# A two-layer graph network on one Trainium2 core: where the nodes are finished, and which engine runs an unused branch's GELU

## The chip, the cores and the metric

The kernel runs on one core of one Trainium2 chip. The core's engines work side by side and meet only at semaphores: TensorE (PE in a profile: matmul, and its weight loads as PEld), VectorE (DVE), ScalarE (ACT), GpSimd (POOL) and SyncE (SP), which here only issues DMA transfers. The metric is the device time of one execution in microseconds (us). The kernel before has a median of 4388.27 us over three runs (4384.02 to 4390.1).

## The reference

There are 6250 nodes of 128 features and 206250 edges, sorted by destination (33 a node on average: 200000 drawn at random, and one self loop a node). Layer 0 is attention over edges and a feed-forward network, layer 1 a convolution over the same edges:

```python
# layer 0
m = leaky_relu(xl[src] + xr[dst] + edge_attr @ W_e, 0.2)
alpha = softmax of einsum(m, att) over the edges of each dst
h = layer_norm(x + segment_sum(xl[src] * alpha, dst) + b_att, g1, be1)
x = _layernorm(x + layer_norm(h + gelu(h @ W1 + b1) @ W2 + b2, g2, be2))
# layer 1, w00.. from a small network on edge_attr_8
n0, n1 = segment_sum(products of w, feat[src], edge_attr_4, dst)
y = cos * self(x) + sin * (n0, n1) @ W2
out = _layernorm(x + y)
```

All arithmetic that matters here is in float32.

## The kernel before, in words

Edges are taken in 403 groups of 512 (four tiles of 128). `program` calls stages one after the other, each a block in which every engine has its own instruction stream; a block ends when all of them have.

1. `set_up` makes the tables `xl` and `xr` and compares the destinations with fixed due groups. Its result `on_time` (with the test that no group spans too many nodes) goes into the flag `narrow`.
2. `attention` runs over the 403 groups. `by_width` branches on `narrow`: the narrow branch (`wins == 1`) has one window of nodes per group, the wide one (`wins > 1`) four. In the narrow branch the node updates of the first 14 x 384 nodes are done inside the loop as jobs (`job_on_pe`, `job_on_act`, `job_on_dve`): by then no later edge reaches those nodes. In the wide branch the jobs come after the loop. ScalarE's stream does not branch: its in-loop GELUs run in either case, and after its loop it runs `job_on_act(act, AFTER, ...)` for all 14 jobs with 4 GELUs each (L667). In the narrow branch TensorE opens these 56 with one `pe.sem_inc(hidden_ready, FC * JOBS)`, and what they write is not read.
3. `update_nodes` does the remaining nodes in two batches of 512.
4. `convolution` is the second loop. GpSimd gathers four tiles of rows per group by indirect DMA (L219) into a ring of eight groups; the gather of group k waits for `vals_ready` of group k-8. VectorE builds one-hot selectors (L1490) and the products (L1517 to L1528), ScalarE scales (L1465), TensorE makes the weights (L1441 to L1451) and sums by destination (L1434), and VectorE adds the sums to `acc` (L1503, L1505). A step of a stream works on several groups at once (TensorE on k to k-4, VectorE on k-3 and k-5).
5. `finish_nodes` comes after the whole loop, 13 batches of up to 512 nodes: TensorE turns `acc` (L1582) and multiplies (L1573, L1574), ScalarE copies the turned sums (L1595), VectorE adds, measures and normalises (L1614 to L1636), GpSimd takes the power -0.5 (L1604), SyncE stores.

The order in each engine's stream is that of the source: `steps` calls a body for every step, and nothing is reordered.

## Time and profile before

| | |
|---|---|
| median of three runs | 4388.27 us (4384.02 to 4390.1) |
| the profiled execution | 4350.94 us, of which the span from first to last instruction is 4348.8 us |
| busy in the span | PE 3377.7 us (78%), PEld 2309.2 (53%), DVE 3207.4 (74%), ACT 1823.7 (42%), POOL 3162.2 (73%) |
| instructions | PE 15016, DVE 10018, ACT 5130, POOL 3264 |
| mean granted TensorE clock | 0.947 of full |

Every time inside the kernel comes from the one profiled execution, which was 37.3 us (0.9%) shorter than the median of the timed runs. Busy shares are averages over stages with different limits; which engine is waited for must be read stage by stage. An engine's time may look idle in the page when it only issues a DMA, since issuing is not counted as busy for SP.

### The profile page before, as it was taken

The page shows a single profiled execution, that of the slowest core. Times are in us where ns is not written, and L with a number is a line of the kernel's source. Part 1 is how long each engine was busy: PE and PEld are TensorE (multiplying, and loading weights), DVE is VectorE, ACT ScalarE, POOL GpSimd, SP SyncE. Part 2 cuts the span into 40 slices and gives each one's busy share as a digit, 9 for nine tenths or more (in the row PEclk, how much of TensorE's full clock was granted, in tenths as well). Part 3 has the DMA queues.
Part 4 walks back from the last instruction along what each step waited for, and adds up shares of the span by engine and source line. Part 5 has one row for each costly group of instructions (what it writes and reads, how often), then busy time and mean ns, then how long its engine had stood idle before and what let it go on. Part 6 is the DMA issues. An engine that isn't in the chain of part 4 may idle for free. (4 is left out here: it accounts for less than half of the span.)

```text
span 4348.8 us, 64316 instructions
## 1 busy us (share of the span) xinstructions
PE 3377.7 (78%) x15016; PEld 2309.2 (53%) x15016; DVE 3207.4 (74%) x10018; ACT 1823.7 (42%) x5130; POOL 3162.2 (73%) x3264
## 2 busy tenths in 40 slices
PE   2878788877788878888567878777888877787776
PEld 2445455554455555554345556555555555555555
DVE  4557677777777767776567788788777787787877
ACT  1455565555555556555722222222222222222222
POOL 5677777777777777777267777777777777777773
PEclk7999999999998999999789999999999999999998
DMA  6655555555555555555112222222222222222221
GB/s 196 187 144 142 142 146 146 143 143 149 143 146 142 141 141 150 146 143 146 58 39 56 55 55 56 55 55 56 55 55 55 56 56 55 56 56 55 56 55 50
DMA packets 327847, 432.36 MB, mean 99 GB/s; under 512 B 132339, under 2 KB 217543, under 8 KB 327336
## 3 DMA queue, kind: packets, MB, share of 16 engines
q0 software_dynamic: 103168, 211.49, 18.6%
q1 hardware_dynamic: 224008, 216.62, 17.7%
q8 instruction: 131, 2.15, 0.2%
q14 instruction: 252, 2.06, 0.2%
q10 hardware_dynamic: 288, 0.04, 0.0%
HBM read 411.20 MB, written 16.65 MB: 98 GB/s over the span
## 5 line engine op out<-in xcount | busy, mean ns | idle before, releaser
L219 POOL DMA_INDIRECT ahead_rows<-feat,ahead_idx x1612 | 1580.8, 981 | 502.1 <-issue 490.7
L176 POOL DMA_INDIRECT ring_rows<-xl,ring_idx x1612 | 1542.6, 957 | 536.5 <-issue 514.8
L1434 PE MATMUL conv_sums_ps<-conv_vals,conv_onehot 128*128 128x256 f32 x3224 | 851.3, 409 | 415.0 <-DVE conv_vals L1528 414.9
L1465 ACT ACTIVATE conv_scaled<-conv_w_ps,c_xT 128x64 f32<-128x64 f32 x1612 | 374.9, 315 | 1451.5 <-PE conv_w_ps L1441 1451.5
L1434 PEld LDWEIGHTS conv_sums_ps<-conv_vals,conv_onehot 128*128 128x128 f32 x3224 | 604.4, 197 | 646.1 <-DVE conv_vals L1528 560.9
L1050 DVE SCALAR_TENSOR_TENSOR attn_leaky<-attn_pre_ps,c_b_r,attn_fifth 128x512 f32<-128x512 f32 x403 | 301.6, 748 | 431.8 <-ACT attn_fifth L930 424.7
L879 PE MATMUL attn_sums_ps<-attn_msg,attn_onehot 128*128 128x136 f32 x3224 | 478.4, 295 | 158.7 <-DVE c_acc_attn L985 155.3
L930 ACT ACTIVATE attn_fifth<-attn_pre_ps,c_b_r 128x512 f32<-128x512 f32 x403 | 276.2, 685 | 758.3 <-PE attn_pre_ps L870 748.1
L1517 DVE TENSOR_TENSOR c_W<-ahead_rows,c_xT 128x384 f32<-128x384 f32 x403 | 225.0, 558 | 407.8 <-DMA ahead_rows<-feat,ahead_idx 407.8
L879 PEld LDWEIGHTS attn_sums_ps<-attn_msg,attn_onehot 128*128 128x128 f32 x3224 | 427.0, 201 | 185.7 <-issue 177.9
L934 ACT ACTIVATE attn_far<-c_iota,c_dst_pos 128x128 f32<-128x128 f32 x1612 | 510.2, 390 | 0.6
L858 PE MATMUL attn_pre_ps<-c_xT,c_W_e 128*128 128x512 f32 x806 | 428.2, 613 | 51.8 <-DMA attn_xr_win<-xr_parts 51.8
L847 PE MATMUL attn_logit_ps<-attn_leaky,attn_att_pad 128*96 128x512 f32 (+2 forms) x806 | 439.2, 628 | 0.0
L1441 PE MATMUL conv_w_ps<-c_Wp,conv_hid 128*128 128x256 f32 x1612 | 436.3, 395 | 0.0
L870 PEld LDWEIGHTS attn_pre_ps<-c_ident,ring_rows 128*128 128x128 f32 x1612 | 191.8, 142 | 402.8 <-DMA ring_rows<-xl,ring_idx 302.9
L870 PE MATMUL attn_pre_ps<-c_ident,ring_rows 128*128 128x128 f32 x1612 | 253.9, 280 | 188.7 <-DMA ring_rows<-xl,ring_idx 188.4
L1490 DVE TENSOR_SCALAR conv_onehot<-c_iota,c_dst_pos 128x128 f32<-128x128 f32 x1612 | 363.6, 297 | 0.8 <-DVE c_acc_conv L1480 0.8
L1441 PEld LDWEIGHTS conv_w_ps<-c_Wp,conv_hid 128*128 128x128 f32 x1612 | 325.2, 202 | 51.5 <-ACT conv_hid L1471 1.0
L1451 PE MATMUL conv_hid_ps<-ahead_radial,c_mlp 16*128 16x256 f32 x806 | 280.7, 427 | 21.9 <-PEq L1063 21.9
L937 ACT ACTIVATE attn_onehot<-attn_far,c_one 128x512 f32<-128x512 f32 x403 | 290.9, 722 | 14.1 <-PE attn_sums_ps L879 1.0
L858 PEld LDWEIGHTS attn_pre_ps<-c_xT,c_W_e 128*128 128x128 f32 x806 | 154.4, 197 | 255.0 <-issue 200.1
L1044 DVE TENSOR_TENSOR attn_msg<-ring_rows,attn_turn_ps 128x512 f32<-128x512 f32 x403 | 271.9, 675 | 0.0
(214 smaller groups left out, 4505.9 us busy)
## 6 DMA issues: line engine op xcount, KB each, us to landing
c_xT<-in_attrT SPq DMA_DIRECT2D x403, 256.0 KB
attn_rel<-rel_group SPq DMA_DIRECT2D x403, 126.0 KB
ring_rows<-xl,ring_idx POOLq DMA_INDIRECT x1612
ahead_rows<-feat,ahead_idx POOLq DMA_INDIRECT x1612, 2.6
attn_xr_win<-xr_parts SPq DMA_DIRECT2D x403, 31.5 KB
ahead_radial<-in_radial_halves SPq DMA_DIRECT2D x101, 64.0 KB, 2.0
attn_limit<-limit SPq DMA_DIRECT2D x403, 16.0 KB
xr_parts<-set_parts SPq DMA_DIRECT2D x13, 384.0 KB, 3.4
```

What stands on the lines that cost most here:

```text
L176: pool.indirect_dma_start(self.rows[:, b, t, :], None, self.q["xl"][:, :], bass.IndirectOffsetOnAxis(ap=self.idx[:, s.slot(2), j * TG + t: ...
L219: pool.indirect_dma_start(self.rows[:, k.slot(U), t, :], None, self.q["feat"][:, :], bass.IndirectOffsetOnAxis(ap=self.idx[:, bass.ds(k.in ...
L847: nc.tensor.matmul(logit_ps[0:n * H, s.slot(2), :], att_pad[:, lo:lo + n * H], leaky[:, g.slot(2), :], start=j == 0, stop=j == n - 1).then ...
L858: nc.tensor.matmul(pre_ps[:, g.slot(2), :], sb["W_e"][:, :], attrT[:, b, :], start=True, stop=False)
L870: last = nc.tensor.matmul(pre_ps[:, g.slot(2), t * P:(t + 1) * P], xl_rows[:, g.slot(NX), t, :], ident[:, :], is_transpose=True, start=Fal ...
L879: last = nc.tensor.matmul(to, onehot[:, g.slot(2), t, :], msg[:, g.slot(2), t, :, :].rearrange("p h o -> p (h o)"), start=wins > 1 or t == ...
L934: nc.scalar.activation(far[:, t, :], sb["iota"][:, :], ACT.Abs, bias=sb["dst_pos"][:, bass.ds(g.index(TG, t), 1)], scale=-1.0).then_inc(fa ...
L1050: nc.vector.scalar_tensor_tensor(out=leaky[:, z.slot(2), :], in0=pre_ps[:, z.slot(2), :], scalar=sb["b_r"][:, 0:1], in1=fifth[:, z.slot(2) ...
L1434: last = nc.tensor.matmul(to, onehot[:, g.slot(2), t, :], vals[:, g.slot(2), t, :], start=wins > 1 or t == 0, stop=wins > 1 or t == TG - 1)
L1441: last = nc.tensor.matmul(w_ps[:, g.slot(2), c:TG:2, :], hid2[:, g.slot(2), c * P:(c + 1) * P], sb["Wp"][:, :, :], start=True, stop=True)
L1465: nc.scalar.activation(scaled[:, g.slot(2), t, :], w_ps[:, g.slot(2), t, 0:2 * MUL], ACT.Copy, scale=edge4[:, bass.ds(g.index(TG, t), 1), ...
L1490: last = nc.vector.tensor_scalar(onehot[:, g.slot(2), t, :], sb["iota"][:, :], sb["dst_pos"][:, bass.ds(g.index(TG, t), 1)], None, ALU.is_ ...
```

## The change

The ScalarE instructions after its attention loop are gone, with the `sem_inc` that opened them. In the wide branch the GELU of those jobs is now computed by VectorE with a rational approximation of erf (`gelu_on_dve`, 19 chained instructions and a last one for each chunk).

`finish_nodes` is gone. Its work is in `convolution`: for j = 0 to 10 in the narrow branch the pieces of batch j stand in the steps from 33 (j+1) + 8 on: TensorE's three (`fin_on_pe`: turn the first half, turn the second half, multiply) at offsets 0, 2 and 4, VectorE's four (`fin_on_dve`: two copies out of PSUM, add and measure, normalise) at offsets 1, 3, 5 and 6. Batch 11 stands in the last four steps and batch 12, of one tile, behind the loop. The reciprocal root is made on VectorE by three Newton steps (12 small chained instructions instead of GpSimd's one), the copies by VectorE instead of ScalarE. The result is normalised in place in `resid`, and SyncE stores all of it after its last radial load. `set_up` compares 12 further due groups and makes `narrow` false if one of them is late.

```diff
+FN = NB * P
+FIN_JOBS = -(-N // FN)
+FIN_EVERY = -(-E * FN // (N * GE))
+FIN_AFTER = 3
...
-                if done.at >= 1:
-                    act.wait_ge(gelu_ready, done.back(1).index(FC, c + 1))
...
-                    if wins == 1 and not k.turns and k.at == G + 3:
-                        pe.sem_inc(hidden_ready, FC * JOBS)
...
             steps(act, G, PEEL, U, TAIL, body, END, True)
-            for n in range(JOBS):
-                for u in range(U):
-                    job_on_act(act, AFTER, Step(JOBS + n), u)
...
                             job_on_dve(dve, AFTER, Step(0, i, 1, True), lambda: dve.wait_ge(acc_steps, 2 * wins * G), u)
+                            if U_HIDDEN <= u < U_HIDDEN + FC:
+                                gelu_on_dve(dve, AFTER, Step(JOBS, i, 1, True), u - U_HIDDEN, Step(0, i, 1, True))
...
+        def fin_settled(j):
+
+            return G if j == FIN_JOBS - 1 else (j + 1) * FIN_EVERY + FIN_AFTER
+
+        def fin_pieces(step):
+
+            found = []
+            for j in range(FIN_JOBS - 1):
+                u = step - fin_settled(j) - TAIL
+                if fin_settled(j) + TAIL + 7 <= G + TAIL:
+                    found += [(j, u // 2, None)] if u in (0, 2, 4) else []
+                    found += [(j, None, {1: 0, 3: 1, 5: 2, 6: 3}[u])] if u in (1, 3, 5, 6) else []
+                elif 0 <= u < 4:
+                    found.append((j, u if u < 3 else None, u))
+            return found
+
+        def fin_on_pe(pe, j, piece, settled):
+
+            if piece == 0:
+                pe.wait_ge(acc_steps, settled)
+            if piece < 2:
+                at_least(pe, fin_dve, j * FDS + FAT["turned0"] if piece else (j - 1) * FDS + FAT["turned1"])
+                for n, t in enumerate(fin_tiles(j)):
+                    last = nc.tensor.transpose(turn_ps[:, n, :], acc[:, t, piece * D:(piece + 1) * D], sb["ident"][:, :])
+            else:
+                pe.wait_ge(fin_dve, j * FDS + FAT["turned1"])
+                for n, t in enumerate(fin_tiles(j)):
+                    nc.tensor.matmul(out_ps[:, n, :], turned[0][:, n, :], sb["W_convA"][:, :], start=True, stop=False)
+                    last = nc.tensor.matmul(out_ps[:, n, :], turned[1][:, n, :], sb["W_convB"][:, :], start=False, stop=True)
+            last.then_inc(fin_pe, 1)
+
+        def fin_on_dve(dve, j, piece):
...
+            if piece < 2:
+                dve.wait_ge(fin_pe, j * FPS + (PE_TURN0, PE_TURN1)[piece])
+                at_least(dve, fin_pe, (j - 1) * FPS + PE_OUT)
+                nc.vector.tensor_copy(turned[piece][:, 0:n, :], turn_ps[:, 0:n, :]).then_inc(fin_dve, 1)
+            if piece == 2:
+                dve.wait_ge(fin_pe, j * FPS + PE_OUT)
+                nc.vector.tensor_tensor(v, out_ps[:, 0:n, :], v, ALU.add).then_inc(fin_dve, 1)
...
             steps(sp, G, PEEL, U, 0, body, written_out=True)
+            for j in range(FIN_JOBS):
+                sp.wait_ge(done_ready, j + 1)
+                if (j + 1) * FN <= N:
+                    sp.dma_start(out[j * FN:(j + 1) * FN, :].rearrange("(t p) f -> p t f", p=P), resid[:, j * NB:(j + 1) * NB, :]).then_inc(stored, 16)
...
-def finish_nodes(nc, sb, q, out, ahead):
...
-                finish_nodes(nc, sb, q, out, ahead)
```

ScalarE's stream between the attention loop and the second loop, before (each row is one or more instructions with their line; `attn_far` and `attn_onehot` are the loop's selectors, `upd_` tiles those of `update_nodes`):

```order
L934 ACTIVATE attn_far<-c_iota,c_dst_pos 128x128 x4
L937 ACTIVATE attn_onehot<-attn_far,c_one 128x512
L667 ACT_TABLE_LOAD
L667 ACTIVATE c_xT<-attn_pre_ps,c_b 128x384 x56
L502 UNCONDITIONAL_BRANCH
L1226 UNCONDITIONAL_BRANCH
L1243 ACTIVATE upd_hT<-upd_hT_ps,c_norm_columns 128x512
L1234 ACTIVATE c_acc_conv<-upd_hidden_ps,c_b 128x512 x4
```

The same place now, with the changed kernel's own line numbers (L994 was L934, L1293 was L1234):

```order
L994 ACTIVATE attn_far<-c_iota,c_dst_pos 128x128 x4
L997 ACTIVATE attn_onehot<-attn_far,c_one 128x512
L516 UNCONDITIONAL_BRANCH
L1285 UNCONDITIONAL_BRANCH
L1302 ACTIVATE upd_hT<-upd_hT_ps,c_norm_columns 128x512
L1293 ACT_TABLE_LOAD
L1293 ACTIVATE c_acc_conv<-upd_hidden_ps,c_b 128x512 x4
```

The 56 GELUs are gone, and the load of the GELU's table stands before the first GELU of `update_nodes`.

TensorE's stream at the end of the second loop's narrow branch, before (`conv_w_ps` and `conv_hid_ps` are the edge network, `conv_sums_ps` the sums of a group):

```order
L1434 MATMUL conv_sums_ps<-conv_vals,conv_onehot 128x256 x4
L1441 MATMUL conv_w_ps<-c_Wp,conv_hid 128x2x128 x2
L1447 MATMUL conv_hid_ps<-conv_hid,c_mlp 128x256
L1434 MATMUL conv_sums_ps<-conv_vals,conv_onehot 128x256 x4
L1441 MATMUL conv_w_ps<-c_Wp,conv_hid 128x2x128 x2
L1434 MATMUL conv_sums_ps<-conv_vals,conv_onehot 128x256 x8
```

The same place now (L1597 was L1434; `conv_turn_ps` holds turned sums, `conv_out_ps` the product for the output):

```order
L1597 MATMUL conv_sums_ps<-conv_vals,conv_onehot 128x256 x4
L1604 MATMUL conv_w_ps<-c_Wp,conv_hid 128x2x128 x2
L1501 MATMUL conv_turn_ps<-c_ident,c_acc_conv 128x128 x4
L1597 MATMUL conv_sums_ps<-conv_vals,conv_onehot 128x256 x4
L1501 MATMUL conv_turn_ps<-c_ident,c_acc_conv 128x128 x4
L1597 MATMUL conv_sums_ps<-conv_vals,conv_onehot 128x256 x4
L1505 MATMUL conv_out_ps<-c_W_convA,c_W 128x128
L1506 MATMUL conv_out_ps<-c_W_convB,c_node_rows 128x128
```

Batch 11's turns stand between the sums of the last groups; after the rows shown come its other three tiles and batch 12.

VectorE's stream at the same place now (L1673 and L1675 were L1503 and L1505; before, the two additions of each of the last groups followed one another with nothing between):

```order
L1698 TENSOR_TENSOR conv_vals<-conv_dot,conv_w_ps 128x4x32
L1521 COPY c_node_rows<-conv_turn_ps 128x512
L1666 TENSOR_LOAD c_tile_block
L1666 ISA x2
L1673 ISA
L1673 SCALAR_TENSOR_TENSOR c_acc_conv<-conv_sums_ps,c_keep,c_acc_conv 128x256
L1675 ISA
L1675 SCALAR_TENSOR_TENSOR c_acc_conv<-conv_sums_ps,c_pass_on,c_acc_conv 128x256
L1524 TENSOR_TENSOR c_acc_attn<-conv_out_ps,c_acc_attn 128x4x128
L1527 BN_STATS conv_stats<-c_acc_attn 128x6 x4
```

So VectorE adds batch 11's product before it adds the last group's sums.

## Rows read from the trace of the kernel before

**Rows 1.** The page; groups show count, busy us, mean ns, idle before and releaser.
```profile
span 4348.8 us, 64316 instructions
...
L219 POOL DMA_INDIRECT ahead_rows<-feat,ahead_idx x1612 | 1580.8, 981 | 502.1 <-issue 490.7
L176 POOL DMA_INDIRECT ring_rows<-xl,ring_idx x1612 | 1542.6, 957 | 536.5 <-issue 514.8
```

**Rows 2.** Waits in the second loop, 2230 to 4280 us: total us, times, longest.
```profile
POOL ahead_rows L219 <- issue: 485.8, 1594, 0.3
PE conv_sums_ps L1434 <- DVE conv_vals L1528: 413.1, 353, 2.9
DVE c_W L1517 <- DMA ahead_rows<-feat,ahead_idx: 406.6, 394, 1.8
```

**Rows 3.** Timeline of ACT at attention's end: start us, us, what.
```profile
2125.61 1.28 ACT L667 ACT_TABLE_LOAD   x1
2126.91 26.52 ACT L667 ACTIVATE c_xT<-attn_pre_ps,c_b 128x384 f32<-128x384 f32 x56
```

**Rows 4.** Timeline of DVE there; in brackets the idle time before.
```profile
2128.90 0.35 DVE L985 SCALAR_TENSOR_TENSOR c_acc_attn<-attn_sums_ps,c_pass_on,c_acc_attn 128x136 f32 x1
2153.74 0.52 DVE L1294 TENSOR_SCALAR c_W_convA<-c_W_convA 128x128 f32<-128x128 f32 x1 [24.49 <-PEq L502]
```

**Rows 5.** Timeline of ACT: first GELU of update_nodes, first table load of the loop.
```profile
2168.60 0.69 ACT L1234 ACTIVATE c_acc_conv<-upd_hidden_ps,c_b 128x512 f32<-128x512 f32 x1 [2.17 <-PE upd_hidden_ps L1198]
...
2224.16 1.28 ACT L1475 ACT_TABLE_LOAD   x1 [22.56 <-PE conv_hid_ps L1451]
```

**Rows 6.** Windows: length; PE, PEld, DVE, ACT, POOL busy; PEclk; DMA share; GB/s.
```profile
2153.70:2203.90 50.20, 26.11 (x112) 16.77 (x112) 29.42 (x95) 9.44 (x14) 24.25 (x16) 0.77 0.31 106
4287.10:4348.80 61.70, 38.94 (x312) 37.18 (x312) 40.58 (x182) 13.31 (x13) 13.14 (x13) 0.88 0.19 53
```

**Rows 7.** Groups by line from 4287 us on, columns as in rows 1.
```profile
L1573 PE MATMUL fin_conv_ps<-c_W_convA,fin_sumT 128*128 128x128 f32 x104 | 21.1, 285 | 5.8 <-DVE fin_v L1614 5.8
...
L1582 PE MATMUL fin_sumT_ps<-c_ident,c_acc_conv 128*128 128x128 f32 x104 | 15.3, 296 | 4.6 <-PEq L1367 3.5 <-ACT fin_sumT L1595 1.1
...
L1614 DVE TENSOR_TENSOR fin_v<-fin_conv_ps,c_acc_attn 128x512 f32<-128x512 f32 x13 | 9.0, 691 | 12.6 <-PE fin_conv_ps L1574 10.4 <-issue 1.7
```

**Rows 8.** Timeline of DVE and POOL in one attention job's normalising.
```profile
1966.82 0.17 DVE L686 TENSOR_SCALAR attn_spread<-attn_moments 128x3 f32<-128x3 f32 x1
...
1968.90 0.95 POOL L176 DMA_INDIRECT ring_rows<-xl,ring_idx  x1 [0.30 <-issue]
...
1969.14 0.16 DVE L698 SCALAR_TENSOR_TENSOR attn_rstd<-attn_error,attn_rstd 128x3 f32<-128x3 f32 x1
1969.33 0.88 DVE L704 TENSOR_SCALAR attn_v<-attn_v,attn_moments,attn_rstd 128x128 f32<-128x128 f32 x3
```

**Rows 9.** Timeline of all engines at the loop's end.
```profile
4278.03 1.29 POOL L219 DMA_INDIRECT ahead_rows<-feat,ahead_idx  x1 [0.30 <-issue]
...
4278.61 0.87 DVE L1490 TENSOR_SCALAR conv_onehot<-c_iota,c_dst_pos 128x128 f32<-128x128 f32 x4
...
4281.51 0.56 DVE L1517 TENSOR_TENSOR c_W<-ahead_rows,c_xT 128x384 f32<-128x384 f32 x1 [1.24 <-DMA ahead_rows<-feat,ahead_idx]
...
4283.72 0.28 DVE L1528 TENSOR_TENSOR conv_vals<-conv_dot,conv_w_ps 128x128 f32<-128x128 f32 x1
...
4284.06 1.99 PE L1434 MATMUL conv_sums_ps<-conv_vals,conv_onehot 128*128 128x256 f32 x8 [1.73 <-DVE conv_vals L1528]
...
4286.61 0.47 DVE L1505 SCALAR_TENSOR_TENSOR c_acc_conv<-conv_sums_ps,c_pass_on,c_acc_conv 128x256 f32 x1
```

**Rows 10.** Timeline of SP: the last radial loads, and the last store.
```profile
4170.12 61.57 SPq L213 DMA_DIRECT2D ahead_radial<-in_radial_halves  x4
...
4345.90 0.28 SPq L1654 DMA_DIRECT2D out<-fin_done  x1
```

**Rows 11.** The source line L219: landing of its transfers.
```profile
DMA to landing us min/median/max: 2.4/2.6/4.6
```

## What the change does to the time

> **What bounds the kernel now.** I read the page first. GpSimd's gathers are its two costliest groups: 1612 in each loop, with idle time that nothing but issuing fills [rows 1]. In the second loop the gathers take 981 ns and about 0.305 us of issue each (485.8 us in 1594 gaps), so a group of four costs 4 x 1.286 = 5.15 us, and 403 groups 2075 us. The waits of that loop say the same from the other side [rows 2]: GpSimd waits for no engine, while VectorE waits 406.6 us in 394 groups for gathered rows, 1.03 us each, and TensorE 413.1 us for VectorE's products. The reader is to see a loop in which GpSimd sets the pace and VectorE and TensorE each have about 1.03 us of room per group.
>
> Then I read the two places where no gather runs. At attention's end the timeline of ScalarE shows a table load and 56 GELUs from 2125.61 to 2153.43 us [rows 3]. VectorE finished its last addition at 2129.25 and began the next stage at 2153.74, after 24.49 us of idling [rows 4]. What ends last there is ScalarE, with work whose output nobody reads. After the second loop the last addition ends at 4286.61 + 0.47 = 4287.08 [rows 9], and the span ends at 4348.8: 61.7 us of `finish_nodes`, in which no engine is busy for more than 41 us and GpSimd for only 13 [rows 6].
>
> **The change part by part.**
>
> ScalarE's 56 GELUs. The next stage began 0.3 us after ScalarE's end (2153.43 to 2153.74). Without them the last to end is VectorE, at 2129.25, so the next stage begins at 2129.55: -24.2 us. The wide branch, with VectorE's GELU in it, is not executed, provided `narrow` holds (last rival). The table load goes with the 56 but comes back before the first GELU of `update_nodes`, as the order shows. There ScalarE waited 2.17 us for TensorE before that GELU, but a load that stands behind the wait is not hidden by it: at the second loop's start the load of 1.28 us begins after 22.56 us of waiting for a matmul, when that matmul is done [rows 5]. The whole stage waits for this GELU, so +1.3 us (bounds 0 and 1.3).
> The Trainium skill (ScalarE: Activation LUTs, What ACT_TABLE_LOAD costs) puts a change of tables at the load plus a drain of about 1.38 us, 2.66 us together, by which this term would be +2.7. The trace does not show the drain: the load takes 1.28 us and the next instruction starts 0.02 us behind it (2125.61 + 1.28 to 2126.91) [rows 3].
>
> `update_nodes` comes 24 us sooner after TensorE's idling. Its clock there was 0.77 of full, with 26.11 us of PE busy [rows 6]. TensorE now idles 24 us less before it, and at full clock 26.11 x 0.23 = 6 us could go. The order of events gives no reason why the granted clock must stay up, so I take 0, with bounds -6 and 0.
>
> `set_up` gets two small VectorE instructions. A small TENSOR_SCALAR takes 0.17 us [rows 8], so +0.3 us (bounds 0 and 0.3).
>
> Batches 0 to 10 in the loop. VectorE's cost for one: add, measure and normalise are the old stage's 40.58 us over 13 batches [rows 6], 3.1 us. The two copies out of PSUM are new to it; nearest is the addition of the same 128x512 from PSUM, 691 ns [rows 7]: 1.4 us. The root is a chain like the attention jobs' own: from 1966.82 to 1969.33, 2.5 us for 12 instructions, of which one is already counted [rows 8]: 2.3 us. Together 6.8 us a batch, in 33 groups that leave 33 x 1.03 = 34 us. TensorE's cost is 38.94 / 13 = 3.0 us, also against 34 us. So both fall behind for some seven groups and catch up long before the next batch. What decides is whether GpSimd notices. The gather of group k waits for the products of k-8. The last group's first gather began 3 x 1.25 before 4278.03, at 4274.3 [rows 9]. The products of group 394, which it had to wait for, were done eight groups before 4284.0, at 4242.8. There are 31 us of slack, and a delay of 6.8 us does not reach it. In these steps TensorE makes each piece while VectorE is a step behind, so the waits that are added find their work done or lose about a microsecond within the same lag. Behind the waiting VectorE instruction stand only the next group's one-hot and additions; what TensorE waits for there has the same slack. Cover: the gathers' 5.15 us a group. If it were gone, the 12 batches would cost 12 x 6.8 = 82 us.
>
> The gathers themselves. VectorE's work can lengthen them: the last gather, 1.29 us against a mean of 0.98, ran beside four one-hots [rows 9], and the mean of this loop, 981 ns, is 24 ns above that of the first, where one-hots are made elsewhere [rows 1]. Over a group that is 0.1 us for four one-hots. The normalising instruction is of the same kind, four to a batch, so 12 x 0.1 = 1.2 us; but beside a whole chain of an attention job a gather took 0.95 us [rows 8], which says 0. I take +1.0 (bounds 0 and 13; the upper one is 12 times the 1.1 us of one batch's four normalising instructions).
> The Trainium skill (SBUF — State Buffer, Who interferes with whom) speaks against this change: a VectorE `copy` or `tensor_scalar` in a two-port mode holds the port pair shared with GpSimd for the whole instruction, and descriptors of GpSimd's DMAs are not written meanwhile. By that rule every normalising instruction blocks, which is the second rival; by the rows it costs a tenth of that.
>
> The end of the loop. The products of the last group end at 4284.0. Before it VectorE has copied batch 11's first half in time for which it waited anyway (1.24 us idle before L1517 [rows 9]). Now: second copy 0.7 (4284.7); additions of group 401 0.9 (4285.6). TensorE finishes the last sums at 4286.05 and multiplies: 41.7 us over 13 batches (21.1 for L1573 and nearly as much for its partner), 3.2 us (4289.3). VectorE: add, measure and normalise 3.1, last additions 0.9, chain 2.3 (4295.6). Batch 12, one tile: two turns and copies, product, add and measure, then the chain of 2.5. I estimate 5.3 us from the chain plus eight short links of 0.3 to 0.4 (4300.9). The last store took 4348.8 - 4345.9 = 2.9 us [rows 10] (4303.8). So 4348.8 - 4303.8: -45.0 us (bounds -48, at TensorE's full clock throughout, and -41).
>
> The stores. SyncE issues eleven of them only after its last radial load, which lies at about 4231.7 [rows 10], 46 us before the last gather. They are 2.9 MB beside 55 GB/s of gathers. Landing takes 2.6 us and at most 4.6 [rows 11]; 2 us more for some groups is made up in the 1.03 us that each leaves. I take 0 (bounds 0 and 2). The last store waits for nothing but batch 12.
>
> Sum: -24.2 + 1.3 + 0.3 + 1.0 - 45.0 = -66.6 us. The span of 4348.8 becomes 4282.2 and the profiled execution of 4350.94 becomes 4284.3. The timed median stands 37.3 us above the profiled execution; since nothing in the profile says where these are, I carry them over unchanged: 4388.3 - 66.6 = 4321.7.
>
> **The rivals.**
>
> The boundary does not move. If something else ends attention, such as SyncE or a barrier that rows of instructions do not show, the 24.2 us stay and the table load doubles: 4388.3 - 66.6 + 24.2 = 4346. For it speaks only that SyncE's waits are not in a row; against it, that VectorE resumed 0.3 us after ScalarE. Chance 0.04.
>
> The gathers pay for each normalising instruction. 12 x 1.1 = 13 us instead of 1: 4334. For it the gather of 1.29 us, against it the gather beside the attention job. Chance 0.07.
>
> Slower than before: GpSimd is held for all of the VectorE time that is added. The place is the eleven batches in the loop and the twelfth in its last steps, the price 12 x 6.8 = 82 us in place of 1: 4388.3 - 66.6 + 81 = 4403. It decides from (66.6 + 1) / 12 = 5.6 us a batch. It needs either the ring's slack to be far below the 31 us that I read, or every kind of VectorE instruction to stop the gathers; [rows 2] and [rows 8] are against both. Chance 0.03.
>
> The change does not run as it says: one of the 12 new due groups is late, `narrow` is false, and the wide branches run. Each group then has six more additions of 0.47 us [rows 9], 2.8 us against 1.03 us of room, over 400 groups at least 700 us, so above 5000. From the reference's inputs I worked out the first destination of each due group: it lies 47 to 58 nodes past what is needed. Chance 0.01.
>
> **How the numbers follow.** The forecast, 4321.7, has 0.83. With the clock's 6 us and the spread of the timed runs (4 us) below it, and the costlier gathers, the slower landing and a longer end above it, its range is 4311 to 4340. That range holds the second rival too. The rest, 0.10, is the boundary (0.04), the two slow cases (0.04 together) and 0.02 for a gain that is lost in small pieces. A measurement of this kernel can tell about 0.2% (8.8 us) from no change. Faster takes the forecast and the first two rivals: 0.94; same 0.02; slower 0.04.
>
> **What would show it.** ScalarE without an activation between about 2125 and 2140, and VectorE resuming within 1 us of its last addition. The first GELU of the next stage behind a load of 1.28 us. In the second loop GpSimd still waiting for issue alone, mean gather 981 to 985 ns, and VectorE's wait for rows down by about 82 us, to some 325. From the last addition of group 402 to the end 12 to 13 us. The forecast is wrong if GpSimd waits for the products anywhere, if the mean gather rises above 990 ns (15 us in 1612), or if stores late in the loop push the last rows' landing back by more than 3 us.

## The result, and the profile after

The changed kernel takes 4324.22 us (median of 4 runs, 4321.41 to 4328.42) against 4386.15 us for the kernel before (4 runs, 4379.48 to 4390.1): -61.9 us, ratio 0.9875 with the interval 0.9848 to 0.9901. The forecast was 4321.7 us. The profiled execution took 4323.39 us with a span of 4321.6. Before's own profiled execution took 4350.94 us, so the two traces differ by only 27.2 us of span while the timed medians differ by 61.9; what lengthens the second loop in the one trace and not in the other is most of what follows.

The kernels below were timed in four further series; in three of them the mean granted clock of TensorE was 0.81 and the kernel before took 5628 to 5730 us (median), so each kernel is compared only with the runs of the kernel before in its own series.

The page's span and its two costliest groups, which answer to [rows 1]:

```profile
span 4321.6 us, 64148 instructions
...
L228 POOL DMA_INDIRECT ahead_rows<-feat,ahead_idx x1612 | 1617.5, 1003 | 504.6 <-issue 490.3
L185 POOL DMA_INDIRECT ring_rows<-xl,ring_idx x1612 | 1543.4, 957 | 535.6 <-issue 516.1
```

The first loop's gathers are as they were. Those of the second loop, 981 ns before, take 1003 now: 36.7 us more in 1612, and still nothing but issuing in GpSimd's idle time. The waits of the second loop, 2230 to 4280 us, answer to [rows 2]:

```profile
POOL ahead_rows L228 <- issue: 477.5, 1566, 0.3
PE conv_sums_ps L1597 <- DVE conv_vals L1698: 395.6, 310, 4.1
DVE c_W L1687 <- DMA ahead_rows<-feat,ahead_idx: 368.0, 343, 2.9
...
POOL ahead_rows L228 <- DVE conv_vals L1698: 0.6, 2, 0.3
```

GpSimd waited for the products 0.6 us in all: the slack of the ring held. VectorE's wait for rows fell by 39 us and not by 82, because the gathers themselves became longer. The boundary between the two loops answers to [rows 3] and [rows 4]: ScalarE's timeline, then VectorE's.

```profile
2124.20 0.72 ACT L997 ACTIVATE attn_onehot<-attn_far,c_one 128x512 f32<-128x512 f32 x1
2143.37 0.78 ACT L1302 ACTIVATE upd_hT<-upd_hT_ps,c_norm_columns 128x512 f32<-128x512 f32 x1 [18.44 <-PE upd_hT_ps L1275]
2144.16 1.28 ACT L1293 ACT_TABLE_LOAD   x1
2146.31 0.69 ACT L1293 ACTIVATE c_acc_conv<-upd_hidden_ps,c_b 128x512 f32<-128x512 f32 x1 [0.86 <-PE upd_hidden_ps L1257]
```

```profile
2128.30 0.35 DVE L1042 SCALAR_TENSOR_TENSOR c_acc_attn<-attn_sums_ps,c_pass_on,c_acc_attn 128x136 f32 x1
2131.38 0.52 DVE L1353 TENSOR_SCALAR c_W_convA<-c_W_convA 128x128 f32<-128x128 f32 x1 [2.73 <-PEq L516]
```

VectorE resumes 2.73 us after its last addition in place of 24.49. The table load stands ahead of the wait for `upd_hidden_ps`: after 1.28 us of loading ScalarE still waits 0.86 us for TensorE. The stage that follows, up to the first gather of the second loop, answers to the first of [rows 6], and the landing of the loop's transfers to [rows 11]:

```profile
2184.89 1.05 POOL L228 DMA_INDIRECT ahead_rows<-feat,ahead_idx  x1 [10.71 <-DMA feat<-c_acc_conv]
```

```profile
2131.38:2184.89 53.51, 28.65 (x112) 18.24 (x112) 29.22 (x95) 10.73 (x15) 24.28 (x16) 0.69 0.28 100
```

```profile
DMA to landing us min/median/max: 2.4/2.6/4.1
```

The stage is 2.4 us longer than the 51.14 us from VectorE's resuming to the first gather before. The end answers to [rows 9] and [rows 10]: the last gather (GpSimd's timeline), then VectorE's last addition for group 402, and SyncE's last store.

```profile
4295.37 0.95 POOL L228 DMA_INDIRECT ahead_rows<-feat,ahead_idx  x1 [0.30 <-issue]
...
4308.51 0.48 DVE L1675 SCALAR_TENSOR_TENSOR c_acc_conv<-conv_sums_ps,c_pass_on,c_acc_conv 128x256 f32 x1
...
4318.85 0.26 SPq L1572 DMA_DIRECT2D out<-c_acc_attn  x1
```

From the end of that addition to the end of the span are 12.7 us. The three stretches of the two traces, cut at the starts of the first and the last gather of the second loop (us):

| | before | after | difference | forecast |
|---|---|---|---|---|
| to the first gather | 2204.88 | 2184.9 | -20.0 | -22.6 |
| first to last gather | 2073.15 | 2110.5 | +37.3 | +1.0 |
| last gather to the end | 70.8 | 26.3 | -44.5 | -45.0 |

Two of the three are right within 3 us. The middle one is not, against this profile of before.

### The profile page after: what moved, and what is told of

Its sections match the earlier page's. It is cut to its first block and busy times, and to the rows that moved or that the text cites. A ratio compares the mean times of both kernels' runs of the same rounds, so it can differ in the third digit from the quotient of the medians.

```text
span 4321.6 us, 64148 instructions
## 1 busy us (share of the span) xinstructions
PE 3400.2 (79%) x14998; PEld 2321.5 (54%) x14998; DVE 3238.5 (75%) x10180; ACT 1785.1 (41%) x5061; POOL 3186.6 (74%) x3251
## 5 line engine op out<-in xcount | busy, mean ns | idle before, releaser
L228 POOL DMA_INDIRECT ahead_rows<-feat,ahead_idx x1612 | 1617.5, 1003 | 504.6 <-issue 490.3
L1597 PE MATMUL conv_sums_ps<-conv_vals,conv_onehot 128*128 128x256 f32 x3224 | 862.7, 414 | 402.9 <-DVE conv_vals L1698 402.1
L1597 PEld LDWEIGHTS conv_sums_ps<-conv_vals,conv_onehot 128*128 128x128 f32 x3224 | 613.4, 200 | 627.1 <-DVE conv_vals L1698 532.0
L994 ACT ACTIVATE attn_far<-c_iota,c_dst_pos 128x128 f32<-128x128 f32 x1612 | 510.8, 391 | 0.6
```

Source lines behind the costliest of these rows:

```text
L228: pool.indirect_dma_start(self.rows[:, k.slot(U), t, :], None, self.q["feat"][:, :], bass.IndirectOffsetOnAxis(ap=self.idx[:, bass.ds(k.in ...
L994: nc.scalar.activation(far[:, t, :], sb["iota"][:, :], ACT.Abs, bias=sb["dst_pos"][:, bass.ds(g.index(TG, t), 1)], scale=-1.0).then_inc(fa ...
L1597: last = nc.tensor.matmul(to, onehot[:, g.slot(2), t, :], vals[:, g.slot(2), t, :], start=wins > 1 or t == 0, stop=wins > 1 or t == TG - 1)
```

## Experiments

Three explanations of the longer gathers were tested. **Theory A**: a gather that starts beside VectorE's products is held until the group's one-hots are done whenever VectorE goes from one to the other with no idle time. The batches bring this about by making VectorE late; and before's own executions differ by how often it happens. **Rival B**: the added normalising and copying instructions themselves hold gathers. **Rival C**: the gap between before's profile and its timed runs has nothing to do with gathers. The first half of A, VectorE's lateness, is borne out below; the second, the one-hots, is not (see "Which instructions hold the gather").

### What the changed kernel's trace shows

VectorE and GpSimd around the normalising of batch 1 and two groups behind it (group 79 to 80):

```profile
2611.36 1.23 DVE L1552 TENSOR_SCALAR c_acc_attn<-c_acc_attn,conv_moments,conv_rstd 128x128 f32<-128x128 f32 x4
2611.59 0.94 POOL L228 DMA_INDIRECT ahead_rows<-feat,ahead_idx  x1 [0.30 <-issue]
2612.38 0.88 DVE L1660 TENSOR_SCALAR conv_onehot<-c_iota,c_dst_pos 128x128 f32<-128x128 f32 x4
2612.84 1.04 POOL L228 DMA_INDIRECT ahead_rows<-feat,ahead_idx  x1 [0.30 <-issue]
...
2617.93 0.56 DVE L1687 TENSOR_TENSOR c_W<-ahead_rows,c_xT 128x384 f32<-128x384 f32 x1
2618.39 0.29 DVE L1689 TENSOR_TENSOR conv_scal<-conv_w_ps,ahead_rows 128x128 f32<-128x128 f32 x1
2618.59 0.29 DVE L1691 TENSOR_TENSOR conv_dot<-c_W 128x128 f32<-128x128 f32 x1
2618.63 2.42 POOL L228 DMA_INDIRECT ahead_rows<-feat,ahead_idx  x1 [0.30 <-issue]
...
2620.13 0.29 DVE L1698 TENSOR_TENSOR conv_vals<-conv_dot,conv_w_ps 128x128 f32<-128x128 f32 x1
2620.33 0.88 DVE L1660 TENSOR_SCALAR conv_onehot<-c_iota,c_dst_pos 128x128 f32<-128x128 f32 x4
```

Beside the four normalising instructions, of 1.23 us together, the gather takes 0.94 us, and in the whole trace the 20 gathers that overlap such an instruction take at most 0.95: they cost nothing, against rival B. The long gather comes in group 80 (2618.63 us; it ends at 2621.05, just before the one-hots' end at 2621.21 and 0.6 us behind that of the last product at 2620.42), when VectorE has been late for two groups and starts its products with no idle time (no bracket behind the row at 2617.93). A gather of 2.4 us stands in the same place behind each of the eleven batches (groups 47, 80, 113, ... 377). The gathers of these eleven groups are 1.9 us longer each than the same ones in the trace of before, 21 of the 36.7 us; the other 16 are spread over the loop.

### The kernel before, profiled again

> The kernel before, unchanged, profiled once more. Its first profile has gathers of 981 ns in the second loop and an execution of 4350.9 us, 37 us under its own timed median; the changed kernel's has 1003 ns and no such gap. Theory A (the length of the gathers is unsteady in both kernels, and the first profile of before caught a short case): a second profile can come out at up to 4388 us, and then with gathers of up to 981 + 37000/1612 = 1004 ns. Theory C (the gap has nothing to do with the gathers): a longer execution with gathers still at 981 ns, the time elsewhere. Theory B (the change alone lengthens the gathers): 981 ns whatever the execution's time.

Measured: 5725.6 us against 5713.0 in the same series (ratio 1.0006, 0.9976 to 1.0035). None of the forecasts' times applies, but the run shows the hold plainly. The window 3500 to 3530 us, then a piece of VectorE's and GpSimd's timeline in it:

```profile
3500.00:3530.00 30.00, 29.50 (x121) 21.37 (x120) 30.00 (x108) 11.79 (x48) 25.73 (x15) 1.00 0.14 39
```

```profile
3503.71 2.42 POOL L219 DMA_INDIRECT ahead_rows<-feat,ahead_idx  x1 [0.30 <-issue]
...
3505.24 0.92 DVE L1490 TENSOR_SCALAR conv_onehot<-c_iota,c_dst_pos 128x128 f32<-128x128 f32 x4
3506.03 0.50 DVE L1503 SCALAR_TENSOR_TENSOR c_acc_conv<-conv_sums_ps,c_keep,c_acc_conv 128x256 f32 x1
...
3506.44 0.94 POOL L219 DMA_INDIRECT ahead_rows<-feat,ahead_idx  x1 [0.30 <-issue]
...
3507.69 2.42 POOL L219 DMA_INDIRECT ahead_rows<-feat,ahead_idx  x1 [0.31 <-issue]
```

VectorE is busy for all 30.00 us, catching up after it had stood still, and gathers of 2.42 and 0.94 us alternate. The long one starts at 3503.71 beside the products and ends at 3506.13, within 0.1 us of the end of the one-hots (3505.24 + 0.92). That the two ends coincide here does not yet make the one-hots the cause. There is no batch in this kernel's loop, so the hold occurs in the kernel before as well. Mean gather of this run: 1141 ns.

> The kernel before, unchanged, profiled a third time. In its second profile (5727 us) ScalarE and VectorE stood still for up to 31 us at a time with nothing that the trace names, and gathers took 2.42 us each wherever VectorE caught up without a gap. If that belongs to the hour and not to the kernel, this run is back near 4386 us. Theory A (the gathers' length is unsteady): an execution between 4350 and 4390 us whose mean gather in the second loop lies between 981 and 1004 ns in proportion. Theory C: near 4388 us with gathers of 981 ns. Theory B: 981 ns, and an execution near 4351 us.

Measured: 5644.7 us against 5628.4 (1.0024, 0.9995 to 1.0053), mean gather 1156 ns: the same picture, and no answer between A and C.

> The kernel before, profiled once more beside its own runs, which lay between 4346 and 4367 us in the hour of the finer-cut version and between 4379 and 4390 us beside the first result, while its first profile took 4350.9 us. Theory A (its gathers are held in some executions and not in others): an execution above 4360 us has a mean gather above 987 ns in the second loop, about 0.62 ns for each us above 4351, with gathers of 2.0 to 2.6 us later than the loop's start; one near 4351 us has 981 ns and none. Theory C: the mean gather stays at 981 ns whatever the time.

Measured: 5718.7 us against 5729.7 (0.9989, 0.9965 to 1.0013), mean gather 1092 ns. So no profile of before at 4360 us or more exists, and what makes its executions lie at 4346 to 4367 us in one series and 4379 to 4390 in another is not settled.

### One part alone

```diff
-                    if wins == 1 and not k.turns and k.at == G + 3:
-                        pe.sem_inc(hidden_ready, FC * JOBS)
...
-            for n in range(JOBS):
-                for u in range(U):
-                    job_on_act(act, AFTER, Step(JOBS + n), u)
```

> The first part of the change alone: the kernel before without the 56 GELUs on ScalarE and the semaphore increment behind them. By the prediction's step: -24.2 + 1.3 = -22.9 us against before. By the changed kernel's trace the table load is hidden before the wait: about -24 us. If what is saved at the boundary comes back in the loop (TensorE's clock, gathers in another phase): -10 to 0 us. The gathers' length in the second loop should be that of the kernel before by each theory.

Measured: 5685.6 against 5713.0 us (0.9955, 0.9935 to 0.9974): -27 us, interval -37 to -15. What VectorE waited for at the boundary (total us, times, longest), in this kernel and in the second profile of before:

```profile
DVE c_W_convA L1289 <- PEq L502: 2.7, 1, 2.7
```

```profile
DVE c_W_convA L1294 <- PEq L502: 22.6, 1, 22.6
```

> The first part alone once more (the kernel before without the 56 GELUs on ScalarE), since before took 5713 us in the hour of its first run. By the changed kernel's trace the next stage begins 22.4 us sooner (GpSimd's first instruction there 2131.36 in place of 2153.73 us) and the second loop's first gather 20.0 us sooner (2184.89 in place of 2204.88): -20 to -24 us against before, plus or minus what the gathers' length does in either, up to 37 us by the two profiles of before and of the changed kernel. By the prediction's step: -22.9.

Measured: 5701.7 against 5729.7 us (0.9960, 0.9938 to 0.9983): -28 us, interval -36 to -10. Both intervals hold the forecast's -22.9, and the wait of 2.7 us comes back. The gathers' lengths in these runs (1160 and 1154 ns) are those of the catching-up and say nothing about this part.

The other part alone is the changed kernel with these lines put back:

```diff
+                if done.at >= 1:
+                    act.wait_ge(gelu_ready, done.back(1).index(FC, c + 1))
...
+                    if wins == 1 and not k.turns and k.at == G + 3:
+                        pe.sem_inc(hidden_ready, FC * JOBS)
...
+            for n in range(JOBS):
+                for u in range(U):
+                    job_on_act(act, AFTER, Step(JOBS + n), u)
```

> The second part alone: the changed kernel with the 56 GELUs on ScalarE put back. By the prediction's steps: +1.0 + 0.3 - 45.0 = -43.7 us against before. If the batches in the loop lengthen gathers as the changed kernel's profile has it against the first of before (+36 us) and before's own timed runs do not have this: about -10 us. Theory A (before's timed runs have long gathers too): -38 to -44 us. In its profile the long gathers stand at the same place of each period of 33 groups as in the changed kernel, if the batches make them.

Measured: 5661.6 against 5713.0 us (0.9903, 0.9877 to 0.9929): -55 us by the ratio, interval -70 to -41. The forecast of -43.7 is inside, the "-10" of a kernel that pays all 36 us is outside. From the end of the last addition to the end of the span this kernel takes 12.8 us, where the three further profiles of before take 61.6 to 61.9: that is the gain at the loop's end. Its long gathers do not stand at one place of each 33 groups, as the changed kernel's do, but where VectorE catches up. In this kernel's loop TensorE, ScalarE and VectorE stand still for up to 34, 31 and 22 us at a time, under which some of GpSimd's extra time may be free, so the run bounds the cost of longer gathers only here.

### All batches behind the loop

```diff
-                    if wins == 1:
-                        for j, _, piece in fin_pieces(k.index()):
-                            if piece is not None:
-                                fin_on_dve(dve, j, piece)
...
-                for j in range(FIN_JOBS - 1 if wins == 1 else 0, FIN_JOBS):
+                for j in range(FIN_JOBS):
```

(and the same for TensorE)

> The changed kernel with all 13 batches made behind the loop, one after the other, none in it. What the loop hides comes due: 12 batches of 6.8 us of VectorE alone, 10 with the hops between engines, so 82 to 120 us more than the changed kernel, less what the gathers get back. Theory A: the long gathers at one place of each 33 groups are gone, mean gather 3 to 20 ns under the changed kernel's 1003. Theory B (each normalising or copying instruction of VectorE holds a gather): the same place is clean, mean gather 981, 36 us given back, so 46 to 84 us more than the changed kernel. Theory C: 1003 ns stays.

Measured: 5793.5 against 5713.0 us (1.0131, 1.0097 to 1.0164), so +75 us against before, and 132 us more than the kernel above, which has the batches in the loop and 24 us of GELUs besides. From the end of the last addition of the loop to the end of the span, with the 13 batches one after another:

```profile
5658.74:5812.10 153.36, 67.46 (x294) 57.84 (x294) 79.45 (x342) 0.00 (x0) 0.00 (x0) 0.62 0.07 22
```

11.8 us a batch: more than the 6.8 to 10 of the expectation. VectorE is busy for 6.1 us of them and TensorE, at 0.62 of its clock, for 5.2 in place of the 3.0 of the prediction, and here the two mostly take turns. The cover that the loop gives the batches is real. Its mean gather, 1131 ns, lies among those of its series (1108 to 1160), so it does not tell A from B.

### The changed kernel again, and the batches in finer pieces

> The changed kernel, unchanged, beside the kernel before of the same hour, for the whole change against the two parts measured in the first call (-26 and -55 us). If the parts add up: -75 to -85 us. By the changed kernel's own timing: -62 us (ratio 0.9875). If the parts share a gain: under -62 us.

Measured: 4316.0 against 4364.4 us (0.9902, 0.9871 to 0.9932): -48 us, less than in the first pair, and not the sum of the parts of another series (-27 and -55 us of 5713). Before's seven runs in this series lie at 4346 to 4367 us, the changed kernel's four at 4315 to 4319. The changed kernel is steadier between the two series (medians 4324 and 4316) than before (4386 and 4364). In before's two shortest runs (4346 and 4349 us) the mean granted clock was 0.949, in its five others 0.935 to 0.943. No trace of these five exists, so whether the clock, the gathers or both make them longer is open.

The finer pieces (`scale` is two of the four normalising instructions; the main lines of the edit):

```diff
...
-                    found += [(j, None, {1: 0, 3: 1, 5: 2, 6: 3}[u])] if u in (1, 3, 5, 6) else []
+                    fine = {1: [0], 3: [1], 5: ["v"], 6: ["stats"], 7: ["moments"], 8: [("root", 0)], 9: [("root", 1)], 10: [("root", 2)], 11: [("scale", 0)], 12: [("scale", 1)]}
+                    found += [(j, None, fine[u])] if u in fine else []
...
```

> The changed kernel with the pieces of a batch on VectorE cut finer and laid over steps 1, 3 and 5 to 12, so that none adds more than 0.9 us to a group that has 1.03 us to spare. Theory A: VectorE never has to catch up, so the gathers of 2.42 us at one place of each 33 groups are gone, 10 x 2 to 3 = 20 to 30 us less than the changed kernel (less where TensorE itself makes VectorE catch up). Rival B (each of the added instructions holds a gather for its own length): no difference, within 5 us. Rival C (nothing to do with gathers): no difference.

Measured: 4298.9 us (4293.1 to 4302.3) in the same series: 0.9859 of before (0.9828 to 0.9890), and 17 us less than the changed kernel, whose four runs lie above all four of this one. The loop's gathers, of the changed kernel in this series and of the finer pieces:

```profile
L228 POOL DMA_INDIRECT ahead_rows<-feat,ahead_idx x1612 | 1612.6, 1000 | 503.0 <-issue 490.6
```

```profile
L228 POOL DMA_INDIRECT ahead_rows<-feat,ahead_idx x1612 | 1597.0, 991 | 504.2 <-issue 489.9
```

15.6 of the 17 us are the gathers: the eleven groups behind the batches take 17.4 us less, all others together 1.8 us more. Gathers above 1.9 us are 22 where they were 30; behind the batches, four of the eleven places still have one, of 1.97 to 2.19 us, and five batches have one of 2.03 to 2.41 us one to three groups earlier. The same instructions are issued, only no more than about 1 us of them in a group: what costs is that VectorE becomes late, as theory A has it, and not the instructions. The forecast of 20 to 30 us was somewhat too high. This version beats both kernels.

### Which instructions hold the gather

One comparison of two tensors in place of the four one-hots:

```diff
-                        for t in range(TG):
-                            last = nc.vector.tensor_scalar(onehot[:, g.slot(2), t, :], sb["iota"][:, :], sb["dst_pos"][:, bass.ds(g.index(TG, t), 1)], None, ALU.is_equal)
-                        last.then_inc(onehot_ready, 1)
+                        nc.vector.tensor_tensor(onehot[:, g.slot(2), :, :], bc(sb["iota"][:, :], 1, TG), bc(sb["dst_pos"][:, bass.ds(g.index(TG), TG)], 2, P), ALU.is_equal).then_inc(onehot_ready, 1)
```

> The changed kernel with the four one-hots of a group as one VectorE instruction that compares two tensors (TENSOR_TENSOR with broadcast operands, 512 columns) instead of four TENSOR_SCALARs. Theory A with TENSOR_SCALAR as the one that holds: no gathers of 2.42 us, as in the version with ScalarE. If any VectorE work without a gap holds gathers: they stay at 2.42 us. The instruction itself may take 0.6 to 1.1 us against 0.87 for the four.

Measured: 4412.3 us in the same series as the last two (1.0129 of before, 1.0096 to 1.0162), 96 us more than the changed kernel. GpSimd and VectorE behind a batch:

```profile
2793.96 2.44 POOL L228 DMA_INDIRECT ahead_rows<-feat,ahead_idx  x1 [0.30 <-issue]
...
2795.50 0.28 DVE L1696 TENSOR_TENSOR conv_vals<-conv_dot,conv_w_ps 128x128 f32<-128x128 f32 x1
2795.70 0.68 DVE L1659 TENSOR_TENSOR conv_onehot<-c_iota,c_dst_pos 128x512 f32<-128x512 f32 x1
...
2796.30 0.47 DVE L1671 SCALAR_TENSOR_TENSOR c_acc_conv<-conv_sums_ps,c_keep,c_acc_conv 128x256 f32 x1
```

The comparison is shorter (0.68 us against 0.88), and the holds of 2.4 us are as long and as many: 29 gathers above 1.9 us against 30 in the changed kernel of this series. So the hold does not hang on TENSOR_SCALAR. It ends at 2796.40, with the comparison (2796.38), but also 0.62 us behind the last product (2795.78). What is new are gathers of about 1.43 us: 258 are above 1.3 us against 49, and 224 end 0.82 us behind the end of the comparison. The mean rises to 1054 ns, 87 of the 96 us: a comparison of two tensors lengthens gathers that the four one-hots leave alone. By the Trainium skill (SBUF — State Buffer, Who interferes with whom) a TENSOR_SCALAR in a two-port mode can keep descriptors from being written; a tensor_tensor with both inputs in SBUF contends with GpSimd's reads but, as the skill infers, not with the writing of descriptors. The rows show gathers of 0.94 us beside the normalising TENSOR_SCALARs and the longer ones beside tensor_tensors, so the first rule does not explain them; which of GpSimd's accesses is in the way no run here shows.

The one-hots on ScalarE, behind its GELUs, and taken out of VectorE's stream:

```diff
...
+                    for t in range(TG):
+                        nc.scalar.activation(onehot[:, g.slot(2), t, :], sb["iota"][:, :], ACT.Abs, bias=sb["dst_pos"][:, bass.ds(g.index(TG, t), 1)], scale=-1.0).then_inc(far_ready, 1)
+                    act.wait_ge(far_ready, g.uses(1, TG))
+                    nc.scalar.activation(onehot[:, g.slot(2), :, :], onehot[:, g.slot(2), :, :], ACT.Relu, bias=sb["one"][:, :], scale=-1.0).then_inc(onehot_ready, 1)
...
```

> The changed kernel with the four one-hots of a group made on ScalarE (4 of 0.39 and 1 of 0.72 us, as in the first loop) instead of on VectorE. Theory A, as it stands after the second profile of before (a gather that falls among VectorE's products is held until the group's one-hots, 2.42 us, when VectorE works without a gap, and the one-hots take part in it): no gather over 2 us, mean near 945 ns, 30 to 90 us less than the changed kernel where TensorE is not in the way. Rival B (the products hold the gather whatever comes behind them, or the normalising instructions do): gathers of about 2.4 us stay where VectorE catches up, the mean stays within 15 ns of the changed kernel's. If the products alone hold: the gathers get shorter by the 0.9 us of the one-hots, about 1.5 us instead of 2.42.

Measured: 5480.9 us (1.2556 of before, 1.2498 to 1.2614; three runs of 5462 to 5486 us, and a fourth of 18336 us that is left out and has no trace). The one-hots stand behind the GELUs in ScalarE's stream, so TensorE's sums wait for them, and the group takes 8.0 us. But the source line of its gathers (durations in ns; minimum, median, maximum) reads:

```profile
L228 POOL DMA_INDIRECT ahead_rows<-feat,ahead_idx x1612: 938/944/1320, 2183.2 to 5392.1; - x180
its engine sat idle before it (us, times) until:
  DVE conv_vals L1700: 1279.0, 386
```

1600 of 1612 gathers take 960 ns or less, with all the batches' copies, roots and normalising instructions still on VectorE (22 gathers overlap a normalising one, of 0.95 us at most): rival B is refuted. VectorE idles over half of this loop, so this run does not single out the one-hots. The same instructions ahead of `conv_scaled` in ScalarE's order:

> The changed kernel with the one-hots on ScalarE again, now ahead of conv_scaled in ScalarE's order instead of behind the GELUs, so that TensorE's sums need not wait for them. ScalarE's work for a group becomes 3.8 us, under the 5.0 us of four gathers. Theory A (only gathers beside VectorE's one-hots are held): every gather near 945 ns, with VectorE busy most of the time now, so 4 x (0.945 + 0.305) = 5.0 us a group and 85 to 90 us less than the changed kernel. If the gathers of 945 ns in the first version came from VectorE's idling (it was busy a good third of the loop): means of 970 to 1000 ns again, and 0 to 50 us less. If ScalarE's new work delays TensorE: slower than the changed kernel, with GpSimd waiting for conv_vals.

Measured: 5649.6 against 5729.7 us (0.9880, 0.9840 to 0.9919; a sixth run, of 11966 us and without a trace, is left out), -69 us by the ratio. The changed kernel is not in this series, so what the version would gain over it is open. VectorE's and GpSimd's timeline where VectorE catches up (from 3549.99 to 3554.7 it has less than 0.05 us of idle time at a stretch):

```profile
3549.99 0.48 DVE L1675 SCALAR_TENSOR_TENSOR c_acc_conv<-conv_sums_ps,c_keep,c_acc_conv 128x256 f32 x1 [0.54 <-PE conv_sums_ps L1598]
...
3551.50 0.94 POOL L228 DMA_INDIRECT ahead_rows<-feat,ahead_idx  x1 [0.31 <-issue]
...
3552.74 1.24 POOL L228 DMA_INDIRECT ahead_rows<-feat,ahead_idx  x1 [0.30 <-issue]
...
3554.29 1.27 POOL L228 DMA_INDIRECT ahead_rows<-feat,ahead_idx  x1 [0.30 <-issue]
```

Here gathers beside the products take 0.94 to 1.27 us. Elsewhere in the same loop, with no one-hots on VectorE, one takes 2.23:

```profile
3465.16 2.23 POOL L228 DMA_INDIRECT ahead_rows<-feat,ahead_idx  x1 [0.30 <-issue]
...
3466.50 0.28 DVE L1700 TENSOR_TENSOR conv_vals<-conv_dot,conv_w_ps 128x128 f32<-128x128 f32 x1
...
3467.66 0.48 DVE L1675 SCALAR_TENSOR_TENSOR c_acc_conv<-conv_sums_ps,c_keep,c_acc_conv 128x256 f32 x1 [0.89 <-remote]
```

It ends at 3467.39, 0.61 us behind the last product, while VectorE idles. Six of 1612 are like this one, of 2.23 to 2.36 us, where before's three profiles of such series have 124 to 203 above 1.9 us. So one-hots on VectorE are not needed for the hold, and the second half of theory A falls.

What the long gathers have in common can be counted over all 14 traces, which have 1343 above 1.9 us. Products here are a group's TENSOR_TENSORs from `c_W` to the `conv_vals` that reads `conv_w_ps` (rows 2617.93 to 2620.13 above), about 2.5 us. Every one started 0.66 to 1.14 us behind the start of a group's products, and ended 0.61 to 0.92 us behind the end of the last product. In the two versions without the four one-hots it is 0.61 to 0.63 throughout, in the others about 0.62, 0.79 or 0.91, so the four one-hots add 0.3 us at most. And of the gathers that started 0.65 to 1.05 us behind the products' start, none of 447 was held where VectorE idled for more than 0.05 us just before the products or among them, and 1314 of 1440 where it did not. That is VectorE's lateness in numbers: a late VectorE finds its rows landed and starts its products without a pause. Products also lengthen gathers that are not held: in the changed kernel's trace the 452 gathers that overlap no product take 949 ns on the mean and the other 1160 take 1025, in the second profile of before 945 and 1299.

In this version 79 of 95 such gathers met idling VectorE, which waited for ScalarE's part (236 waits before `conv_scal`), and 6 of the other 16 were held. That is the main reason why it has so few. Whether the one-hots raise the share of held ones (6 of 16 here, 182 of 193 in the second profile of before) is open.

The mean is 1003 ns against 1092 to 1156. The 945 that A named did not come: besides the six, 243 of 1612 gathers take 1.1 to 1.5 us.

## Why the prediction was right, and where it was not

The time came out within 2.5 us of the forecast, but one term of the sum was wrong by more than ten times its size in the traces, and a base that nobody had explained made up for it. The mechanism at the boundary and at the loop's end was right; that the time fits so closely is luck as far as the runs show.

- **The boundary, -24.2**: measured -22.4 (GpSimd and VectorE begin the next stage at 2131.4 in place of 2153.7). The mechanism is shown by the part alone (-27 and -28 us, and the wait down from 22.6 to 2.7). The size missed 1.8 us: between VectorE's last addition and its resuming lie 2.73 us, which before were hidden under ScalarE's work, and I had taken the 0.3 us that followed ScalarE's end; the last addition itself came 0.6 us sooner.
- **The table load, +1.3**: measured 0. From VectorE's resuming to the first GELU are 14.9 us in both traces. The step that said "a load that stands behind the wait" read the wrong order out of [rows 5]: here the load runs ahead of the wait and is hidden by it. The lower bound was right.
- **TensorE's clock in `update_nodes`, 0 (-6 to 0)**: outside the bounds. The granted clock of the stage is 0.69 where it was 0.77, TensorE is busy 28.65 us where it was 26.11, and the stage is 2.4 us longer. The difference lies near the stage's end: from 2173.4 to 2180.4 us the clock is 0.50, its lower level, and at the same place of before (2195.7 to 2202.7) it was 0.92. Less idling before a stage gave no faster clock in it.
- **Batches in the loop, 0**: right. GpSimd waited 0.6 us for products.
- **The gathers, +1.0 (0 to 13)**: this is the term that was mis-sized. Against the profile of before it is +36.7 us. Against before's timed runs it follows from the medians and the other two stretches: -61.9 + 20.0 + 44.5 = +2.6 us in the first pair, and -48.5 + 20.5 + 46.2 = +18 in the second (4314.2 - 4289.6 = 24.6 us from last gather to end there). I priced the instructions that could hold a gather and left out the lateness they cause, which carries gathers into the stretch of the products where they are held; the sentence "both fall behind for some seven groups and catch up long before the next batch" named the cause and gave it no price. The stated sign of failure, a mean gather above 990 ns, did appear. The rival of the normalising instructions named 13 us for the wrong reason: gathers beside them take 0.95 us at most, and the finer pieces keep all of them and lose 15.6 us.
- **The end of the loop, -45.0**: measured -44.5, with 12.7 us from the last addition where 12 to 13 were named. The part alone has 12.8 in place of 61.6 to 61.9.
- **The stores, 0**: landing took at most 4.1 us, as before (4.6).
- **The time**: 4324.2 against 4321.7; for the profiled execution the same sum gave 4284.3, and it took 4323.4. The base of 37.3 us between before's profile and its timed median was carried over as unexplained and fixed. It was not fixed: the changed kernel's profile and timed median agree within 1 us. That its gathers are 36.7 us longer than in before's profile suggests that before's timed runs had them too, and that the forecast was right on the times while wrong on the traces. This is argued, not shown: none of the three further profiles of before fell near 4386 us, and beside before's 4364 us the gain was 48 us and not 66.6.

One reading behind the mis-sized term was wrong too. The prediction laid the gather of 1.29 us [rows 9] to the one-hots beside it. It started at 4278.03 beside the group's products, and ended at 4279.32, 0.63 us behind the last of them:

```profile
4278.41 0.28 DVE L1528 TENSOR_TENSOR conv_vals<-conv_dot,conv_w_ps 128x128 f32<-128x128 f32 x1
```

What had to be priced was how many gathers start beside products, and where in them.

## What to carry to other kernels

Work laid beside a bounding engine's stream must be cut so that no step adds more than that step's idle time, even where the buffers have slack for it: the same VectorE instructions cost 17 us less in ten pieces than in four. Before a profile serves as the base of a sum, hold its own time against the timed runs of the same kernel; a gap as large as the effect means that the base has a term that the sum does not know. An end that coincides with an instruction's end does not make it the cause: compare the distance to the instructions before it, and take the suspect out. And when an engine's tail is removed, look for the wait that it had hidden (2.73 us here), not for the gap behind its end.

## What the runs showed of the hardware

- A GpSimd gather of 0.94 us that starts 0.66 to 1.14 us behind the start of VectorE's run of products takes 1.9 to 2.6 us in most cases if VectorE has no idle time just before and among them (1314 of the 1440 that start by 1.05 us), and never if it has (1.08 us at most in 447). It ends 0.61 to 0.92 us behind the last product. Four one-hots behind the products add 0.3 us at most, and none are needed (six gathers of 2.23 to 2.36 us without them). Beside four normalising instructions a gather keeps its 0.94 us. The mechanism is open.
- One comparison of two tensors (128x512, 0.68 us) lengthens gathers to about 1.43 us, 224 times of 1612. Beside four one-hots by TENSOR_SCALAR and no product, 114 gathers of the second profile of before take 1.04 us at most.
- A table load of 1.28 us ran before a wait of its instruction and was hidden by it.
- With before at 5628 to 5730 us, ScalarE stood still for up to 31 us at a time in the second loop, VectorE for up to 30 and TensorE for up to 34, while GpSimd waited for products for 12 us at most. What starts these waits is open.
